# Keys and values projected ahead of a sampling by pairs of images, the maximum of the point softmax subtracted by TensorE, and the plain vo behind the attention

## What is computed

```
xn = group norm of x, one group per channel
q  = wq . xn                                  # 1x1 convolution
off = depthwise 5x5 convolution of q, stride 4, two groups of 16 channels: 4x4 points
off = gelu(off / sqrt(var over 16 channels) * ln_w);  off = w_off . off     # 3 rows
pos = reference points + tanh(off[0], off[1]) / 4
dm  = sigmoid(off[2])
xs  = bilinear sample of xn at pos, times dm              # 16 points per image and group
k, v = wk . xs, wv . xs                                   # 4 heads of 8 channels
bias = bilinear sample of the 31x31 table rpe at (query - pos) / 2
x  = xn + ... : x + wo . (softmax(q.k * scale + bias) . v)         # the point softmax, over 16 points
t  = tokens of x;  t = t + softmax(ln(t) . ln(t)') . ln(t)          # second attention, 256 tokens
t  = t + mixture of 16 experts, each taking its 8 strongest tokens  # first layer, gelu, second layer
```

## Time and profile before

| | us |
|---|---|
| time, median of 3 runs | 62.66 (62.41 to 62.8) |
| time of the profiled execution | 62.32 |
| its span | 60.3 |
| busy PE / DVE / ACT / POOL | 51.2 / 37.2 / 29.0 / 23.0 |
| fillers on PE (192) | 14.1 |

### The profile page before, as it was taken

How to read it: one execution, slowest core, us unless ns; L and a number is a source line. 1 busy time by engine, 2 the same in 40 slices (tenths; PEclk the granted TensorE clock), 3 DMA queues, 4 the chain that set the end, 5 groups by cost and what they waited for, 6 DMA issues and landing times.

```text
span 60.3 us, 1440 instructions
## 1 busy us (share of the span) xinstructions
PE 51.2 (85%) x582; PEld 41.8 (69%) x582; DVE 37.2 (62%) x91; ACT 29.0 (48%) x62; POOL 23.0 (38%) x47
## 2 busy tenths in 40 slices
PE   3995996997897899999999978397798998989920
PEld 3994894974686889899898957161286686878800
DVE  3387599937569899099960372477998517740320
ACT  0801051969999405017558752989527227501020
POOL 6040189993879899500420000035400691000000
PEclk9999999999999999999999999999999999999999
DMA  0789931100000000000000000000000000000004
GB/s 0 210 130 277 240 123 46 57 31 8 0 0 0 11 0 0 0 0 0 0 0 0 11 5 5 0 0 0 0 0 0 0 11 0 0 0 0 0 31 143
DMA packets 3926, 2.02 MB, mean 34 GB/s; under 512 B 2640, under 2 KB 3792, under 8 KB 3920
## 3 DMA queue, kind: packets, MB, share of 16 engines
q1 hardware_dynamic: 1424, 1.37, 8.4%
q10 hardware_dynamic: 2496, 0.57, 4.4%
HBM read 1.67 MB, written 0.26 MB: 32 GB/s over the span
## 4 chain that ended last, share of the span: by engine, by line
PE 46%; DVE 18%; ACT 11%; POOL 10%; issue 6%; DMA 4%; DVEq 0%; POOLq 0%; ACTq 0%
PE ps L758 4%; DMA x_sb<-x_rows 4%; PE ps L677 4%; ACT e_tok L631 4%; PE ps L802 3%; PE ps L751 3%; PE ps L823 3%; PE ps L780 3%; DVE e_sum L1091 3%; POOL e_fold L497 2%; DVE taps L999 2%; POOL w_smp L478 2%; DVE off L1001 2%; PE ps L713 2%; PE ps L741 2%
## 5 line engine op out<-in xcount | busy, mean ns | idle before, releaser
L677 PE MATMUL ps<-zeros 128*128 128x128 bf16 x192 | 14.1, 231 | 1.0 <-DVE zeros L976 1.0
L677 PEld LDWEIGHTS ps<-zeros 128*128 128x128 bf16 x192 | 12.9, 105 | 1.6 <-DVE zeros L976 1.0
L522 ACT ACT_TABLE_LOAD x4 | 5.1, 1283 | 1.7 <-PEq L1195 1.6
L497 POOL TENSOR_TENSOR e_fold<-e_tok 128x256 f32<-128x256 f32 x2 | 1.5, 738 | 10.2 <-ACT e_tok L631 10.2
L631 ACT ACTIVATE e_tok<-ps,cst 128x1024 f32<-128x1024 f32 (+1 forms) x5 | 4.4, 941 | 1.4 <-PE ps L838 1.4
L1030 DVE COPY_PREDICATED ps<-over,ps 128x608 f32<-128x608 uint32 (+1 forms) x4 | 3.1, 777 | 0.8 <-PE ps L730 0.7
L838 PE MATMUL ps<-t_t 32*128 32x256 f32 x32 | 2.3, 399 | 1.1 <-ACT e_tok L631 0.9
L730 PE MATMUL ps<-rpe_blk,minus_hat_rel 128*32 128x168 f32 x64 | 2.8, 316 | 0.5 <-DVE minus_hat_rel L1026 0.5
L582 ACT ACTIVATE kv<-ps,cst 128x256 f32<-128x256 f32 x4 | 1.7, 472 | 2.8 <-PE ps L751 2.8
L730 PEld LDWEIGHTS ps<-rpe_blk,minus_hat_rel 128*32 128x32 f32 x64 | 2.0, 142 | 1.3 <-issue 0.9
L431 POOL TENSOR_TENSOR wblk<-wts,cst 128x256 f32<-128x256 f32 x3 | 2.1, 688 | 2.3 <-DMA wts<-weights 2.3
(11 more groups left out here) (180 smaller groups left out, 124.2 us busy)
## 6 DMA issues: line engine op xcount, KB each, us to landing
w_sb<-weight ACTq DMA_DIRECT2D x1, 256.0 KB, 6.7
w_sb<-weight SPq DMA_DIRECT2D x1, 256.0 KB, 5.5
x_nat<-x_rows SPq DMA_DIRECT2D x8, 32.0 KB
wts<-weights SPq DMA_DIRECT2D x1, 192.5 KB, 4.6
cst<-shape_consts SPq DMA_DIRECT2D x1, 192.0 KB, 4.1
x_sb<-x_rows SPq DMA_DIRECT2D x1, 128.0 KB, 2.5
x_sb<-x_rows ACTq DMA_DIRECT2D x1, 128.0 KB, 2.7
cst<-shape_consts SPq DMA_DIRECT2D x1, 128.0 KB, 5.3
```

The costliest lines, as they stand in the source:

```text
L497: return nc.gpsimd.tensor_tensor(e_fold[:, n], e[:, :, 0:M // 2], e[:, :, M // 2:], ALU.add)
L522: nc.scalar.add_instruction(mybir.InstLoadActFuncSet(name=nc.get_next_instruction_name(), act_func_set_id=functions, ins=[], outs=[]))
L677: mm(bank(n_bank, P), zeros[:, :], zeros[:, :], start=True, stop=True)
```

## The change

Keys and values are projected from xn for all 256 pixels (tile `k_tok`, `v_tok`, by token) and sampled afterwards. The sampling is done for pairs of images: 32 columns of the tokens' tile by 32 points, in four column groups of TensorE. A pair's points meet both images' channels, and `copy_heads` keeps, in four instructions, the channels of the head and of the right image of the pair (constant `head` with four columns). So the matmul that shut the gate for other images goes, and the gate's product is made with a hat (`hat_gate`) ahead of the sampling. `wk_s` carries the factor 0.5 of the sigmoid written with tanh. The maximum of the point softmax is subtracted by a matmul with minus identity into the logits' bank, and ScalarE exponentiates from PSUM. In TensorE's program both halves' logits are gathered together. The plain vo is made and copied behind the attention. The number of fillers changes.

```diff
-    "xn_ready": 45, "off_ready": 22, "off_blk_ready": 28, "w_smp_ready": 20, "xs_ready": 8,
-    "d_prob_ready": 0, "prob_copied": 3, "t1_ready": 20, "t1_copied": 7, "t2_ready": 12,
+    "xn_ready": 45, "off_ready": 5, "off_blk_ready": 14, "w_smp_ready": 6,
+    "prob_copied": 3, "t1_ready": 8, "t1_copied": 7, "t2_ready": 12,
...
@@ gpsimd
             pool.wait_ge(weights_loaded[1], 16)
+            link(nc.gpsimd.tensor_scalar(wk_s[:, :, :], wkvo[:, 0], 0.5 * QK_SCALE, None, ALU.mult))
+            for g in range(G):
+                blocks(wblk[:, 1, g], wk_s[:, g].rearrange("p (g o) -> p g o", g=G), G, GC).then_inc(wk_ready, 1)
             pool.wait_ge(const_loaded[2], 16)
...
+            nc.gpsimd.tensor_scalar(minus_ident[:, :], ident, -1.0, None, ALU.mult).then_inc(minus_ident_ready, 1)
...
-            pool.wait_ge(hat_smp_ready, 1)
-            for h in range(NHALF):
-                nc.gpsimd.tensor_tensor(w_smp[:, h], hat_smp[:, h], hat_smp[:, 2], ALU.mult).then_inc(w_smp_ready, 1)
             link(nc.gpsimd.tensor_tensor(tap_both[:, :, :], tap_next[:, :, :], tap_prev[:, :, :], ALU.add))
             nc.gpsimd.tensor_scalar(tap_here[:, :, :], tap_both[:, :, :], -1.0, 1.0, ALU.mult,
                                     ALU.add).then_inc(taps_ready, 1)
+            pool.wait_ge(hat_gate_ready, 1)
+            for h in range(NHALF):
+                nc.gpsimd.tensor_tensor(w_smp[:, h], hat_smp[:, h], hat_gate[:, :], ALU.mult).then_inc(w_smp_ready, 1)
@@ scalar
-            act.wait_ge(xn_turned, 1)
-            nc.scalar.activation(xn_tok[:, :, :, :], xnt_ps, ACT.Copy, scale=0.5).then_inc(xn_tok_copied, 1)
             copy_q(0)
+            copy_q(1)
+            act.wait_ge(ktok_done, 1)
+            nc.scalar.activation(k_tok[:, 0], ktok_ps[0], ACT.Copy).then_inc(ktok_copied, 1)
             act.wait_ge(centered, 1)
...
+            for h in range(NHALF):
+                act.wait_ge(vtok_done, h + 1)
+                nc.scalar.activation(v_tok[:, h], vtok_ps[h], ACT.Copy, scale=0.5).then_inc(vtok_copied, 1)
 
             def copy_heads(w, ready):
 
+                pairs_ps = kv_ps[w].rearrange("p g (t q s n) -> p (g t) q s n", t=NT, s=2, n=N)
+                pairs_sb = kv[:, w].rearrange("p g t k (q s n) -> p (g t) k q s n", s=2, n=N)
                 for hh in range(HG):
-                    nc.scalar.activation(kv[:, w, :, :, hh], kv_ps[w].rearrange("p g (t j) -> p g t j", t=NT), ACT.Copy,
-                                         scale=const("head")[:, hh:hh + 1]).then_inc(ready, 1)
+                    for side in range(2):
+                        nc.scalar.activation(pairs_sb[:, :, hh, :, side], pairs_ps[:, :, :, side], ACT.Copy,
+                                             scale=const("head")[:, 2 * hh + side:2 * hh + side + 1]).then_inc(ready, 1)
 
             act.wait_ge(k_done, 1)
             copy_heads(0, k_ready)
-            act.wait_ge(d_sub_ready, 1)
-            nc.scalar.activation(d_exp[:, 0], d_sub[:, 0], ACT.Exp).then_inc(d_exp_ready, 1)
             act.wait_ge(v_done, 1)
             copy_heads(1, v_ready)
-            act.wait_ge(d_sub_ready, 2)
-            nc.scalar.activation(d_exp[:, 1], d_sub[:, 1], ACT.Exp).then_inc(d_exp_ready, 1)
+            for h in range(NHALF):
+                act.wait_ge(d_sub_done, h + 1)
+                nc.scalar.activation(d_exp[:, h], lg_rows[h], ACT.Exp).then_inc(d_exp_ready, 1)
...
             keep_centred(1)
+            act.wait_ge(vo_done, 2)
+            nc.scalar.activation(vo[:, :, :, :], vo_ps, ACT.Copy).then_inc(vo_copied, 1)
@@ tensor
+            def project(outputs, w, h, done):
+
+                for gi in range(G):
+                    last = mm(outputs[h][:, gi].rearrange("p g o -> p (g o)"), xn[:, gi, h * P:(h + 1) * P],
+                              wblk[:, w, gi].rearrange("p g b o -> p (g b o)"), start=True, stop=True)
+                last.then_inc(done, 1)
+
+            pe.wait_ge(wk_ready, G)
+            project(ktok_ps, 1, 0, ktok_done)
+            keep_busy("off_ready", 7)
+
             pe.wait_ge(const_loaded[1], 16)
-            (turns of xn)
             pe.wait_ge(off_ready, G)
             mm(cen_ps, const("center"), off[:, :], start=True, stop=True).then_inc(centered, 1)
             pe.wait_ge(squared, 1)
             mm(var_ps, const("avg"), off_sq[:, :], start=True, stop=True).then_inc(var_done, 1)
-            (the shutting matmul, L703)
+            project(ktok_ps, 1, 1, ktok_done)
+            keep_busy("off_blk_ready", 6)
...
+            pe.wait_ge(half_tanh_ready, 1)
+            pe.wait_ge(txh_ready, 1)
+            pe.wait_ge(wkvo_ready, G)
+            for h in range(NHALF):
+                project(vtok_ps, 2, h, vtok_done)
+            pe.wait_ge(ktok_copied, NHALF)
             keep_busy("w_smp_ready", 5)
+            for n in (4, 5):
+                mm(bank(n, 2 * P).rearrange("p (g n) -> p g n", g=G), zeros[:, :],
+                   zeros[:, :].unsqueeze(1).to_broadcast([P, G, P]), start=True, stop=True)
+
+            def sample(outputs, tokens, h):
+
+                for gi in range(G):
+                    for g in range(G):
+                        for j in range(4):
+                            rows = slice(32 * j, 32 * j + 32)
+                            last = mm(outputs[rows, g, rows], tokens[:, h, gi, g, rows],
+                                      w_smp[:, h, P * gi + 32 * j:P * gi + 32 * j + 32],
+                                      start=False, stop=(h == NHALF - 1 and gi == G - 1), skip_group_check=True)
                 return last
+            for h in range(NHALF):
+                pe.wait_ge(w_smp_ready, h + 1)
+                last = sample(kv_ps[0], k_tok, h)
+            last.then_inc(k_done, 1)
+            for h in range(NHALF):
+                pe.wait_ge(vtok_copied, h + 1)
+                last = sample(kv_ps[1], v_tok, h)
+            last.then_inc(v_done, 1)
...
             for h in range(NHALF):
                 turn_on(left, 0, h, start=True)
-            pe.wait_ge(part_ready[0], 2)
-            for h in range(NHALF):
-                turn_on(right, 0, h)
-
             pe.wait_ge(part_ready[1], 1)
             for h in range(NHALF):
                 turn_on(left, 1, h)
-            pe.wait_ge(k_ready, HG)
+            pe.wait_ge(k_ready, 2 * HG)
             for h in range(NHALF):
                 for g in range(G):
                     mm(lg_ps[:, h, g].rearrange("p t k j -> p (t k j)"), q_sb[:, g, h * P:(h + 1) * P],
                        kv[:, 0, g].rearrange("p t k j -> p (t k j)"), start=False, stop=False, skip_group_check=True)
-                pe.wait_ge(part_ready[1], 2)
+            pe.wait_ge(part_ready[0], 2)
+            for h in range(NHALF):
+                turn_on(right, 0, h)
+            pe.wait_ge(part_ready[1], 2)
+            for h in range(NHALF):
                 turn_on(right, 1, h)
-                pe.wait_ge(part_ready[0], 3)
+            pe.wait_ge(part_ready[0], 3)
+            for h in range(NHALF):
                 turn_on(here, 0, h)
-                pe.wait_ge(part_ready[1], 3)
+            pe.wait_ge(part_ready[1], 3)
+            for h in range(NHALF):
                 turn_on(here, 1, h).then_inc(logits_done, 1)
 
-            project(1).then_inc(v_done, 1)
+            pe.wait_ge(minus_ident_ready, 1)
+            for h in range(NHALF):
+                pe.wait_ge(d_max_ready, h + 1)
+                mm(lg_ps[:, h].rearrange("p g t k (b n) -> p (g t k b) n", n=N), minus_ident[:, :],
+                   d_max[:, h].unsqueeze(2).to_broadcast([P, 32, N]), start=False, stop=True,
+                   skip_group_check=True).then_inc(d_sub_done, 1)
...
+            combine(voc_ps, woblk_c)          # ahead of the turned probabilities
...
+            combine(vo_ps, woblk)             # behind the attention
             keep_busy("t1_ready", 6)
@@ vector
             (behind wo_c)
+            dve.wait_ge(ktok_done, 2)
+            nc.vector.tensor_copy(k_tok[:, 1], ktok_ps[1]).then_inc(ktok_copied, 1)
...
             link(shifted(0, IMG + 2, over[:, 0, 3:4], 1))
+            dve.wait_ge(half_tanh_ready, 1)
+            dve.wait_ge(hat_smp_ready, 1)
+            stt(out=hat_gate[:, :], in0=half_tanh[:, :], scalar=1.0, in1=hat_smp[:, 2], op0=ALU.add,
+                op1=ALU.mult).then_inc(hat_gate_ready, 1)
             shifted(0, IMG + 1, odd[:, 0:1], 1).then_inc(shifts_done, 1)
...
             link(shifted(1, IMG + 2, over[:, 1, 3:4], 1))
-            dve.wait_ge(sampled, 1)
-            dve.wait_ge(half_tanh_ready, 1)
-            stt(out=xs[:, :, :].rearrange("p g n -> p (g n)"), in0=half_tanh[:, :], scalar=1.0,
-                in1=xs_ps.rearrange("p g n -> p (g n)"), op0=ALU.add, op1=ALU.mult).then_inc(xs_ready, 1)
             shifted(1, IMG + 1, odd[:, 1:2], 1).then_inc(shifts_done, 1)
...
-                link(reduce(d_max[:, h], lg_rows[h], AX.X, ALU.max))
```

(3 more changed lines are left out.)

## The result

| | before | after |
|---|---|---|
| median, us | 62.53 | 63.76 |
| ratio, 95% interval | | 1.0183 (1.0142 to 1.0224) |
| span of the profiled execution, us | 60.3 | 61.2 |
| fillers on TensorE | 192 | 127 |

What follows compares the result with a forecast made beforehand. The bound was taken to change from stage to stage, TensorE holding almost half the chain. Front 0.40, softmax and attention 0.8 and vo 0.19 gave 1.4 on 62.32, 63.7, by the median 64.05, told as 64.0; range 63.0 to 64.6.

Steps and rivals of the forecast that it cites:

- The front: Start to square of offsets: keys' projection waits for GpSimd's weight blocks, square at 10.27 instead of 9.87, +0.40 us.
- the three signs of being wrong: First maximum before 26, subtraction under 0.5, or square of the offsets by 9.9 would show the forecast wrong.
- the rival that I gave a chance of 0.20: Weights land early or the front's wait is hidden: only +1.0, 63.6 us; chance 0.20.
- Middle, -0.12: Sampling stage: VectorE's left, group 1, ends at 22.76 + 0.40 - 0.12 = 23.04.
- The gain at k_done: Sampled keys done at about 21.9 against 22.64; the 0.7 won is lost again waiting for VectorE's left.
- Logits, first half 1.5 later: Both halves' logits reach VectorE together at 27.02; the first half came at 25.51 before.
- Subtraction on TensorE: Point softmax, after the maximum: two passes of 0.87 plus 0.27 for start and end, from 27.72 to 28.86.
- Softmax and attention, +0.8 beyond the front: First half's softmax product at 31.8 instead of 30.56; attention's end +1.2 with the front's 0.40 in it.
- Vo behind, +0.19: Second attention's scores wait for ScalarE's copy of the plain vo, +0.19 us (0 to 0.6).
- TensorE's own work: Rival: TensorE's work from 22.64 on decides, so removed projections make the kernel faster, 61.8 us; chance 0.08.
- The small products: Sampling matmuls run serially, 2.05 each instead of 0.52, giving 66 us; chance 0.05 shared with the clock drop.
- the risk that I gave 0.05: Clock drops in a TensorE hole as fillers go, +1 to +2 us; chance 0.05 shared with serial small products.

Runs made afterwards that it cites:

- the kernel with the hole of 1.84: Changed kernel with halves' logits gathered one after the other and VectorE subtracting the maximum; ratio 1.016 to the kernel before, median 64.33 us.
- that of 2.95: Changed kernel with VectorE subtracting the maximum, both halves' logits still gathered together; ratio 1.044 to the kernel before, median 65.81 us.
- one of 2.42 us: Changed kernel with the DMA of the weights' second part issued behind two constants and the first expert weights; ratio 1.0455 to the kernel before.

## Why the prediction was right

Forecast 64.0 us from 62.66, with 63.0 to 64.6; measured 63.76 against 62.53. From the middle on, the mechanism and the places were as told. The front was not: its term of 0.40 was next to nothing, one of the three signs of being wrong came true (the square by 9.9; it started at 9.80), and with it the rival that I gave a chance of 0.20 and 63.6 us. The measured time lies between forecast and rival and can't tell them apart; the traces do.

- *Front, +0.40*: measured 0.06. This is the term that failed. I took one landing of one execution (6.7) as the next one's; it was 0.4 to 0.5 earlier, a bound that I had named. In the nine profiled executions with this order of the queue GpSimd starts between 6.02 and 6.82, so my 6.8 was at the late end. Late weights cost 1.7 us and the chain of the changed kernel runs over their landing, so the mechanism holds. The changed kernel loads fewer constants, but these stand behind the weights in the queue; whether that made the weights land earlier is not shown.
- *Middle, -0.12*: measured -0.11. The rows that I named give up to 0.16 for it, and I gave no reason for the 0.12. The gain at k_done was lost again at VectorE's left, as told.
- *Logits, first half 1.5 later*: from the square to the first maximum 16.79 against 15.64, +1.15; I had 16.76, the 1.5 having the front in it. Shown by undoing it (-0.85 us) and by doing it alone (+1.6 us).
- *Subtraction on TensorE*: from the maximum's end to the result 1.25 (27.28 to 28.53), forecast 1.14. The two passes took 1.11, and the hand-over from the maximum 0.14, which I had not counted apart.
- *Softmax and attention, +0.8 beyond the front*: +0.86 at the attention's end.
- *Vo behind, +0.19*: +0.16; and moving it back costs 0.4 in this kernel.
- *Rivals.* TensorE's own work doesn't decide in the changed kernel: it waits 0.66 and 0.29 there. It does decide when the subtraction is put into the kernel before. The small products are not serial. The clock stayed up in the changed kernel, but the risk that I gave 0.05 was near: take the subtraction away and it falls.

The terms beyond the front were forecast at 1.0 together and measured 1.02. With the front's 0.06 that is 1.08, and the ratio's 1.14 (0.9 to 1.4) agrees with it.

## What to carry to other kernels

When a stage ends in one result made of two halves, give the first half to the next engine as soon as it can be had; gathering both first costs nothing on the gathering engine and a stage's length behind it. Before pricing a gain at one input of a product, find the other input's time: here keys 1.1 us earlier gave 0.1, because the table's branch on VectorE came no sooner. And an edit that takes work off TensorE needs a look at the hole it leaves, as the granted clock can fall there and cost more than the work did.

## What the runs showed of the hardware

- The granted clock fell to 1.2 GHz behind holes of 1.84 and 2.95 us of TensorE inside the kernel, and the 16 passes of the attention took 3.25 to 3.55 us instead of 2.02. In the kernel with the hole of 1.84 the mean granted clock was below 0.99 in five of six runs, with that of 2.95 in six of six, and with one of 2.42 us in two of seven. Behind one of 0.95 us it did not fall. Thirty fillers in the hole of 1.84 kept it up.
- Matmuls of 128x32 weights and 32 columns in four column groups start 0.009 us apart (62 in 0.73). The Trainium skill (TensorE: Matmul & The Clock Gate, "Part 1") states a floor of about 25 ns from start to start; these rows don't show it for passes that go to four column groups in turn.
- A matmul of minus identity over 512 fp32 columns, into a bank that already holds the sum, takes 1.11 us from start to result, and two of them in a row take 1.96.
